# Moving matmul operands to other places in SBUF, counted in 64-byte units modulo four, in a one-core graph and attention layer

## The reference, cut to what matters

```
xn  = layernorm(x)
gnn = gather over dst of (xn @ weight), weighted by a softmax of attention sums over src and dst
Q, K, v = elu(xn@Wq)+1, elu(xn@Wk)+1, (xn@Wv)/L          # 8 heads of 32
msg = (Q @ (K^T v)) / (Q . sum K) * L @ Wm ; msg = layernorm(msg)*g1+b1
h   = relu(concat[xn, msg] @ W1) @ W2      # 512 -> 512 -> 256
x   = x + gnn + xn + layernorm(h)*g2+b2
z   = layernorm(x)
out = x + mlp(z; sW1, sW2, sW3) + top-2 of 4 experts(z; eW1, eW2, eW3), gated by softmax(z @ gW)
```

## The kernel before, in words

| tensors | used as | unit before | unit after |
|---|---|---|---|
| `w_hi`, `w_lo` | held under 512 columns, moving with 256 | 2 | 2 |
| `xT0` | moving, 512 | 0 | 2 |
| `xT1` | moving, 512 | 2 | 2 |
| `mT`, `s1` | moving, 512 | 3 | 2 |
| `z` | moving, 512; held under `g` | 3 | 2 |
| `rdenT` over `den_sel` | moving, 512, over held | 1 over 1 | 2 over 2 |
| `scaleT` over `gate_sel` | moving, 512, over held | 3 over 2 | 3 over 3 |
| `g` | moving, 256 | 2 | 1 |
| `h`, `s2_lo` | held under `w`, 256 | 3 | 3 |
| `s2_hi` | held under `w`, 256 | 1 | 3 |
| `wk` over `x1T` | moving, 256, over held | 2 over 3 | 2 over 3 |
| `wx` over `x1T` | moving, 264, over held | 2 and 0 over 3 | 2 over 3 |
| `xr` over `k` | moving, 258, over held | 0 and 2 over 1 | 2 over 3 |

## Time and profile before

### The profile page before, as it was taken

The page is one execution under the profiler, slowest core; times in us unless marked ns, Lnnn a source line. Parts: engine busy times, 40 slices in busy tenths (PEclk is TensorE's granted clock), DMA queues, the critical chain, the costliest instruction groups (busy, mean ns, idle before and its releaser), DMA issues.

```text
span 1326.4 us, 26270 instructions
## 1 busy us (share of the span) xinstructions
PE 1294.6 (98%) x8812; PEld 1121.4 (85%) x8812; DVE 1077.4 (81%) x2641; ACT 731.6 (55%) x1332; POOL 666.7 (50%) x771
## 2 busy tenths in 40 slices
PE   6999999898999999999999999999999999999998
PEld 6999999776888888888888888888888888888886
DVE  6888777978888888888888888888878888888875
ACT  4555555334645655555645655555645655555654
POOL 5777777746444453444444453444544453444421
PEclk9999999999999999999999999999999999999999
DMA  6787767522122221222121220222121220212000
GB/s 208 241 287 246 254 222 235 153 60 74 40 66 57 80 77 27 72 64 80 39 64 56 80 80 24 74 62 80 41 63 56 80 80 24 76 60 71 25 17 24
DMA packets 65460, 123.24 MB, mean 93 GB/s; under 512 B 31725, under 2 KB 36176, under 8 KB 65422
## 3 DMA queue, kind: packets, MB, share of 16 engines
q1 hardware_dynamic: 57422, 109.25, 25.5%
q0 software_dynamic: 8000, 13.53, 4.6%
HBM read 70.41 MB, written 52.32 MB: 93 GB/s over the span
## 4 chain that ended last, share of the span: by engine, by line
PE 88%; DVE 4%; issue 3%; ACT 2%; POOL 1%; POOLq 1%; DVEq 1%; ACTq 0%
PE psum L272 26%; PE psum L273 25%; PE psum L274 25%; PE psum L484 5%; PE psum L676 3%; PE psum L729 1%; PE psum L667 1%; PE psum L566 1%; PE psum L739 1%; PE psum L559 1%; POOLq L1780 1%; DVE s_lo L1516 0%; POOL ag L1842 0%; POOL xg L1840 0%; POOLq L1836 0%
## 5 line engine op out<-in xcount | busy, mean ns | idle before, releaser
L1846 POOL TENSOR_TENSOR h_lo<-relu,h_hi 128x1024 fp32r<-128x1024 f32 (+1 forms) x50 | 118.4, 2369 | 142.1 <-ACT h_hi L998 142.1
L272 PE MATMUL psum<-w_hi,h_hi 128*128 128x256 f32 x588 | 165.7, 282 | 4.9 <-ACT e L1009 3.1
L273 PE MATMUL psum<-w_lo,h_hi 128*128 128x256 f32 x588 | 165.0, 281 | 0.0
L274 PE MATMUL psum<-w_hi,h_lo 128*128 128x256 f32 x588 | 164.9, 281 | 0.0
L1846 POOL TENSOR_TENSOR s_lo<-relu,s_hi 128x512 fp32r<-128x512 f32 x23 | 29.6, 1289 | 206.0 <-ACT s_hi L1099 206.0
L272 PE MATMUL psum<-z_hi,w_hi 128*128 128x512 f32 (+1 forms) x300 | 121.6, 405 | 2.0 <-DVE z_lo L1616 1.1
L272 PE MATMUL psum<-xT_hi,w_hi 128*128 128x512 f32 (+1 forms) x300 | 118.9, 396 | 0.2 <-DVE relu L1556 0.2
L1840 POOL DMA_INDIRECT xg<-table_xt,idx x100 | 100.5, 1005 | 34.9 <-issue 33.2
L272 PEld LDWEIGHTS psum<-w_hi,h_hi 128*128 128x128 f32 x588 | 111.5, 190 | 7.1 <-ACT e L1009 3.3
L997 ACT ACTIVATE relu<-psum,h_bias 128x512 f32<-128x512 f32 (+1 forms) x100 | 67.8, 678 | 88.9 <-PE psum L274 88.8
L273 PE MATMUL psum<-z_lo,w_hi 128*128 128x512 f32 (+1 forms) x300 | 116.6, 389 | 0.0
(11 more groups left out here) (275 smaller groups left out, 4255.9 us busy)
## 6 DMA issues: line engine op xcount, KB each, us to landing
xb<-in_x SPq DMA_DIRECT2D x47, 448.0 KB, 3.9
xT_hi_table<-x1T_hi SPq DMA_DIRECT2D x25, 512.0 KB, 2.8
xT_lo_table<-x1T_lo SPq DMA_DIRECT2D x25, 512.0 KB, 3.6
xT_hi<-xT_hi_table SPq DMA_DIRECT2D x25, 512.0 KB, 3.8
xT_lo<-xT_lo_table SPq DMA_DIRECT2D x25, 512.0 KB, 4.8
table_xt<-xts SPq DMA_DIRECT2D x24, 455.0 KB, 3.0
out<-xmid SPq DMA_DIRECT2D x24, 448.0 KB, 2.9
xb<-in_x SPq DMA_DIRECT2D x47, 64.0 KB, 4.1
```

What stands on the lines that cost most here:

```text
L272: pe.matmul(out, wh, xh, start=first, stop=False)
L273: pe.matmul(out, wh, xl, start=False, stop=False)
L274: return pe.matmul(out, wl, xh, start=False, stop=last)
L1846: ptt(out, src, hi, ALU.subtract).then_inc(S[done], 1)
```

## The change

`side` now takes a unit modulo 4 instead of a parity, with up to three filler lines, and the count starts at 2, so that it is the unit of the address. Four names take the place of MOVING and HELD: WIDE = 2 (tensors that move with 512 columns, and the weights), HELD = 3 (held under 256 columns), KEYS = 1 and KEYS_HELD = 2 (`g`, and `z` which is held under it). Some tensors get a side that had none. The pitch of `wx` and `xr` grows from 288 to 320 floats, so that each of their parts starts at the same unit. No instruction is added, removed or moved to another place in an engine's order.

```diff
-MOVING, HELD = 0, 1
+FIRST = 2
+WIDE, HELD, KEYS, KEYS_HELD = 2, 3, 1, 2
-XA_PITCH = KX_PITCH = 288
+XA_PITCH = KX_PITCH = 320
-        used = [0]
+        used = [FIRST]
             lines = -(-4 * math.prod(shape[1:]) // LINE)
-            if side is not None and used[0] % 2 != side:
-                stack.enter_context(nc.sbuf_tensor(name + "_side", [P, LINE // 4], F32))
-                used[0] += 1
+            off = 0 if side is None else (side - used[0]) % 4
+            if off:
+                stack.enter_context(nc.sbuf_tensor(name + "_side", [P, off * LINE // 4], F32))
+                used[0] += off
...
-        w_hi = sb("w_hi", [P, W_TOTAL], F32R, side=MOVING)
-        w_lo = sb("w_lo", [P, W_TOTAL], F32R, side=MOVING)
-        out_bias = sb("out_bias", [P, C], F32R, side=MOVING)
-        gate_sel = sb("gate_sel", [P, 2, P], F32R)
+        w_hi = sb("w_hi", [P, W_TOTAL], F32R, side=WIDE)
+        w_lo = sb("w_lo", [P, W_TOTAL], F32R, side=WIDE)
+        out_bias = sb("out_bias", [P, C], F32R, side=WIDE)
+        gate_sel = sb("gate_sel", [P, 2, P], F32R, side=HELD)
...
-        g_hi = sb("g_hi", [P, CK, C], F32R, side=MOVING)
+        g_hi = sb("g_hi", [P, CK, C], F32R, side=KEYS)
...
-        xT_hi0 = sb("xT_hi0", [P, CK, GR], F32R)
+        xT_hi0 = sb("xT_hi0", [P, CK, GR], F32R, side=WIDE)
...
-        den_sel = sb("den_sel", [P, CK, P], F32R)
+        den_sel = sb("den_sel", [P, CK, P], F32R, side=WIDE)
...
-        rdenT = sb("rdenT", [P, GR], F32R)
+        rdenT = sb("rdenT", [P, GR], F32R, side=WIDE)
...
-        z_hi = sb("z_hi", [P, CK, GR], F32R, side=HELD)
+        z_hi = sb("z_hi", [P, CK, GR], F32R, side=KEYS_HELD)
...
-        s1_hi = sb("s1_hi", [P, 2, GR], F32R)
+        s1_hi = sb("s1_hi", [P, 2, GR], F32R, side=WIDE)
...
-        mT_hi = sb("mT_hi", [P, CK, GR], F32R)
+        mT_hi = sb("mT_hi", [P, CK, GR], F32R, side=WIDE)
...
```

More of the change, by code:

```diff
@@ L126, in gps_layer @@
         ident = sb("ident", [P, P])
-        w_hi = sb("w_hi", [P, W_TOTAL], F32R, side=MOVING)
-        w_lo = sb("w_lo", [P, W_TOTAL], F32R, side=MOVING)
-        out_bias = sb("out_bias", [P, C], F32R, side=MOVING)
-        gate_sel = sb("gate_sel", [P, 2, P], F32R)
+        w_hi = sb("w_hi", [P, W_TOTAL], F32R, side=WIDE)
+        w_lo = sb("w_lo", [P, W_TOTAL], F32R, side=WIDE)
+        out_bias = sb("out_bias", [P, C], F32R, side=WIDE)
+        gate_sel = sb("gate_sel", [P, 2, P], F32R, side=HELD)
         gate_w = sb("gate_w", [P, CK, QUAD])
         second_w = sb("second_w", [P, EXPERTS, HEAD_CH])
-        g_hi = sb("g_hi", [P, CK, C], F32R, side=MOVING)
-        g_lo = sb("g_lo", [P, CK, C], F32R, side=MOVING)
+        g_hi = sb("g_hi", [P, CK, C], F32R, side=KEYS)
+        g_lo = sb("g_lo", [P, CK, C], F32R, side=KEYS)
         g2_bc = sb("g2_bc", [R, C])
@@ L169, in gps_layer @@
         row_n = sb("row_n", [R, T, C])
-        xT_hi0 = sb("xT_hi0", [P, CK, GR], F32R)
-        xT_lo0 = sb("xT_lo0", [P, CK, GR], F32R)
+        xT_hi0 = sb("xT_hi0", [P, CK, GR], F32R, side=WIDE)
+        xT_lo0 = sb("xT_lo0", [P, CK, GR], F32R, side=WIDE)
         qf = sb("qf", [P, CK, GR])
@@ L174, in gps_layer @@
         low_rows = sb("low_rows", [P, QUAD + 1])
-        den_sel = sb("den_sel", [P, CK, P], F32R)
+        den_sel = sb("den_sel", [P, CK, P], F32R, side=WIDE)
         ctx1, before_ctx1 = ExitStack(), used[0]
         w_raw = sb("w_raw", [P, W_TOTAL], stack=ctx1)
[L180 to L183, removed]
+        wk_hi = sb("wk_hi", [P, CK, C], F32R, stack=ctx1, side=WIDE)
+        wk_lo = sb("wk_lo", [P, CK, C], F32R, stack=ctx1, side=WIDE)
+        wx_hi = sb("wx_hi", [P, CK, XA_PITCH], F32R, stack=ctx1, side=WIDE)
+        wx_lo = sb("wx_lo", [P, CK, XA_PITCH], F32R, stack=ctx1, side=WIDE)
         x1T_hi = [sb(f"x1T_hi{n}", [P, CK, GR], F32R, stack=ctx1, side=HELD) for n in range(2)]
@@ L196, in gps_layer @@
         xn1 = [sb(f"xn1_{n}", [R, T, C], stack=ctx1) for n in range(2)]
-        xr_hi = [sb(f"xr_hi{n}", [R, T, KX_PITCH], F32R, stack=ctx1, side=MOVING) for n in range(2)]
-        xr_lo = [sb(f"xr_lo{n}", [R, T, KX_PITCH], F32R, stack=ctx1, side=MOVING) for n in range(2)]
+        xr_hi = [sb(f"xr_hi{n}", [R, T, KX_PITCH], F32R, stack=ctx1, side=WIDE) for n in range(2)]
+        xr_lo = [sb(f"xr_lo{n}", [R, T, KX_PITCH], F32R, stack=ctx1, side=WIDE) for n in range(2)]
         kf = [sb(f"kf{n}", [R, T, C], stack=ctx1) for n in range(2)]
@@ L221, in gps_layer @@
         ag = [sb(f"ag{n}", [R, T, HEADS]) for n in range(2)]
-        xT_hi = [xT_hi0, sb("xT_hi1", [P, CK, GR], F32R)]
-        xT_lo = [xT_lo0, sb("xT_lo1", [P, CK, GR], F32R)]
+        xT_hi = [xT_hi0, sb("xT_hi1", [P, CK, GR], F32R, side=WIDE)]
+        xT_lo = [xT_lo0, sb("xT_lo1", [P, CK, GR], F32R, side=WIDE)]
         h_hi = sb("h_hi", [P, 4, GR], F32R, side=HELD)
         h_lo = sb("h_lo", [P, 4, GR], F32R, side=HELD)
-        z_hi = sb("z_hi", [P, CK, GR], F32R, side=HELD)
-        z_lo = sb("z_lo", [P, CK, GR], F32R, side=HELD)
-        s1_hi = sb("s1_hi", [P, 2, GR], F32R)
-        s1_lo = sb("s1_lo", [P, 2, GR], F32R)
+        z_hi = sb("z_hi", [P, CK, GR], F32R, side=KEYS_HELD)
+        z_lo = sb("z_lo", [P, CK, GR], F32R, side=KEYS_HELD)
+        s1_hi = sb("s1_hi", [P, 2, GR], F32R, side=WIDE)
+        s1_lo = sb("s1_lo", [P, 2, GR], F32R, side=WIDE)
         scaleT = sb("scaleT", [P, GR], F32R, side=HELD)
-        mT_hi = sb("mT_hi", [P, CK, GR], F32R)
-        mT_lo = sb("mT_lo", [P, CK, GR], F32R)
+        mT_hi = sb("mT_hi", [P, CK, GR], F32R, side=WIDE)
+        mT_lo = sb("mT_lo", [P, CK, GR], F32R, side=WIDE)
         s2_lo = sb("s2_lo", [P, GR], F32R, side=HELD)
```

## The result

The changed kernel took 1331.8 us in the median of 15 runs (1325.7 to 1333.6), the kernel before, in 15 runs beside it, 1325.9 (1320.9 to 1327.0). The ratio is 1.0039, with a 95% interval of 1.0025 to 1.0053: slower by about 5 us, where 8.4 us less was forecast (1315, in a range of 1308 to 1320). The profiled execution took 1332.01 us with a span of 1330.3, against 1328.16 and 1326.4 before.

The account below looks back on a forecast made before the run. The prediction took the spacing of PE's matmuls as the bound. Gains of 4.0 (512 columns), 3.2 (W2) and 1.2 us (phase 1), 8.4 in all, took the median from 1323.7 to a predicted 1315 us, range 1308 to 1320.

Parts of the forecast that it names:

- What bounds the kernel: Phase 2: PE never waits in turns 3 to 23, so only the spacing of matmuls sets the span.
- The 512-column term: Phase 2 matmuls on `xT0`, `mT`, `z`, `s1` become equal pairs, 2 over 2; 4.0 us gained.
- The mark of 42.25 us a turn: Turn length in phase 2 that the profile after would show if the forecast was right.
- The W2 term: W2 in phase 2 falls into the fast spacing behind eW1 on `z`, now an equal pair; 3.2 us gained.
- The other 256-column sections add nothing to this: Phase 2's 256-column sections besides W2 were priced at nothing, since turns differ by 0.165 us in all.
- Phase 1: `wx` and `xr` at new units gain a quarter of at most 4.7 us: 1.2 us, lower bound nothing.
- A: Rival for all matmuls: placement does not matter, time stays at 1323.7 us; chance 0.09.
- the rule quoted beside it: TensorE has two independent read ports, so loading next weights takes no bandwidth from the running matmul; the change does nothing.
- C: Rival: W2 stays as it is, or `z` is no equal pair because the period exceeds four units; 1318.5 us, chance 0.17.
- D: Rival: phase 1 wins all of its 4.7 us, giving 1311.8 us; chance 0.12.
- B: Rival: phase 2's 256-column sections and `wk` tip into the slow spacing; 4.6 us slower, 1328 us; chance 0.07.
- the two reads collide: In PE, reads of moving and next stationary operand collide at some offsets, about 4 ns in each matmul.

Follow-up runs that it names:

- b_xm: Kernel before with only `xT0` and `mT` moved to unit 2; 1322.3 us in rounds, ratio 0.9952.
- b_z: Kernel before with only `z` moved to unit 2 and `g` to 1; 1325.56 us once, beside 1323.3.
- a_s2: Changed kernel with `s2_hi` back at unit 1; 1333.3 us once, beside 1326.55 of the kernel before.
- b_s2: Kernel before with only `s2_hi` moved, from unit 1 to 3; 1335.1 us once.
- b_x: Kernel before with `xT0`, `mT`, `s1`, `rdenT`, `den_sel` at unit 2; 1324.41 us once; timed in rounds as b_x_timed, 1324.1 us, ratio 0.9971.
- u0_pairs: Layer left out: only matmul triples on zeros, moving unit 2 or 1 over held units 0 to 7; spacings measured, 113.3 to 120.0 ns at 256 columns.
- before_again: Kernel before, unchanged, profiled a second time; its 21 turns took 892.20 us.
- a_mix: Changed kernel with `s2_hi` and `h_lo` at unit 1 and `g_lo` at 3; 1323.7 us in rounds, ratio 0.9969.
- a_gate: Changed kernel with `gate_sel` back at unit 2; 1337.87 us once.
- after_again: Changed kernel, unchanged, run again; 1332.4 us in rounds against the kernel before, ratio 1.0030.

## Why the prediction was wrong

*What bounds the kernel*: right. The whole of the difference in the turns is in the spacing of PE's matmuls, and VectorE's time, 739.83 for 739.60 us, hardly changed. What failed are two terms of the sum: W2, entered with the wrong sign, and the other 256-column sections, entered at nothing.

*The 512-column term*, 4.0 us: right, a little large. 0.141 us a turn are 3.4 us over 24, and the parts are `xT` 1.1 (priced 1.8), `mT` 0.7 (1.0), `z` 1.2 (1.0) and the rest 0.4. The marks came out: 2.72 us for 12 on Wq in even and odd turns. Wq alone gives 1.1 us, nearly all of `xT`. What is missing against the price is not the pairs' own: in b_xm, where `xT0` and `mT` alone move, they gain 1.9 and 1.3 us. In the changed kernel it is missing where sections start afresh. The 12 matmuls on `mT` behind the transposes take 2.850 us (before 2.846, b_xm 2.821), W1 parts 0 and 1 behind the slow `g` 2.764 (before 2.761, b_xm 2.746). In turn 11 the 11 matmuls from 689.87 to 692.40 take 230.0 ns each, and the 12 behind them 226.7. eW1's last 17 take 3.90 us as before, not 3.88. (The mark of 42.25 us a turn was a slip besides: 42.585 less 7.2 / 24 is 42.285.)

*The W2 term*, 3.2 us gained: wrong, and in its sign. "If the entry decides, W2 falls into the fast spacing behind it" was half right. The entry decides, as b_z shows with W2's own operands in place; but the equal pair in front leads into the slow spacing. The step took "fast in front" for "fast behind" on no row at all. W2 in turn 11 before stood behind the same 3 over 2 as in turn 14, so no row told which entry leads where. It measured 0.059 us a turn lost, 1.4 us over 24, close to the bound that the text named (1.6 us), which had as much right to be the value as the gain had.

*"The other 256-column sections add nothing to this"*: the costliest error. It was read from the turns of before, where these sections differ little from turn to turn. That says that they had one spacing there, not that they would keep it. They were all fast, and their being fast hung on things that the change took away. For the output product that is shown in both directions by a_s2 and b_s2: 0.15 us a turn, from one held tensor that 8 of the 40 matmuls read. `g` tips when `z` and `g` alone move (b_z), and also when neither of its operands moves (b_x, b_xm), 0.09 us a turn each time. Together 0.237 us a turn, 5.7 us in the span, entered at nothing.

*Phase 1*, 1.2 us gained: wrong by 1.5 us. `wx` and `xr` over their new pairs have the spacing of before, and the turn is 0.014 us longer. The step scaled 2 over 3 at 256 columns to 258 and 264; no row supported the scaling, and the fact that the step itself named, that half of `wx` stood at 2 over 3 already "and the section is none the faster", spoke against it. The lower bound of nothing was the value to take.

*The rivals.* A falls: the pairs differ by up to 7.5 ns with nothing else changed. And it is the pair that counts: held unit 0 is among the slowest under moving unit 2 (120.0 ns) and among the fastest under moving unit 1 (113.3). So the rule quoted beside it, the Trainium skill, "TensorE: Matmul & The Clock Gate", section "Step-by-step: what each phase is for", does not describe these matmuls: with separate ports that took nothing from each other, u0_pairs would show one spacing for each width. C falls: u0_pairs speaks against its period of eight, `z` at its new place gained 1.2 us, and W2 did not stay as it was; D falls with phase 1. B, at a chance of 0.07, is what happened. It priced 1920 tipped matmuls at 7.9 us against a gain of 4.0, and nearly all of them tipped: 0.296 us a turn, 7.1 us over 24, against 3.4. Only its further 1.9 us for `wk` did not come. It gave 4.6 us and the trace shows 3.9 in the span.

The rounds show some 5.2 us (1325.9 x 0.0039), more than these 3.9. An estimate of the rest: against before_again, where W2 is mostly fast, the difference of the turns would be 897.40 - 892.20 = 5.2 us. If most executions of the kernel before are nearer to that one than to the profiled one, nothing more has to be explained; but only two of them were seen in a trace, so this is not shown.

So what is shown is this. In this kernel a 256-column section of these triples has two spacings, 113.3 to 114 and 117.5 to 118 ns, at the same addresses, and mostly holds the one it is in. Which it gets depends on what ran in front of it, and a held tensor at another unit inside it can throw it into the fast one. Before, `s2_hi` at unit 1 was such a break, among `scaleT`, `s2_lo` and `h` at 3. The change made all held tensors of the output product equal, and it led into W2 and `g` by other entries.

What stays open: why `g` isn't freed by its break in a_mix (only `g_lo` was shifted, a moving tensor, where the breaks that worked were held ones; a held one, `z_lo`, wasn't tried); which of `s1`, `rdenT` and `den_sel` tips `g`; why u0_pairs, on zeros, has 2 over 3 in the slow spacing behind either entry; what makes W2 choose in the kernel before; and what the passage's 107.6 to 120.0 us hang on. In a_s2, a_gate and b_s2 ScalarE waited 12.0 us there before the copy into `g_hi`, elsewhere 6.0 to 7.5, with no cause found; these three were taken side by side on one chip, and the kernel before took 1326.55 us there, without a profile. No run tested what the two reads do inside the engine, so "the two reads collide" remains a picture.

## What to carry to other kernels

A spacing read from a trace belongs to a section with its neighbours, not to its pair of addresses. Where one placement shows two spacings, price every section of that kind at both of them, those whose operands don't move too. Move the tensors of one product at a time and read the spacing of all the others after each step; here the part with the clean rows, two tensors, measured 0.5% faster, and the full scheme cost 0.4%. And take the mark from a stretch in which the bounding engine never waits: 21 such turns of the changed kernel repeated to 0.2 us, where single times of the same kernel lay 8 us apart.

## What was not expected of the hardware

- The effect of the held operand's place repeats after four units of 64 bytes, and the pair that is best at one width is worst at another: 2 over 2 has 226.7 ns at 512 columns, the lowest of the four, and 120.0 at 256, as high as any. 1 over 2, at 256, has 113.3 alone and 117.5 in the changed kernel.
- An equal pair at 512 columns reaches its spacing only after a run-in behind transposes: after the first matmul, seven more at 230.0 ns in u0_pairs and eleven in turn 11 of the changed kernel, then 226.7.
- Two 256-column sections with several others between them can flip together: in b_x_timed, turn 23, the spacings of W2 and of `g` are both the opposite of what they are in the 20 other turns.
- In the passage between the phases, where PE has waits, the granted clock fell from 2.4 to 1.2 GHz, the lower of its two levels, for 3.4 to 17.1 us in all, and in after_again not at all. In the window from 254 to 335 us the profile of the changed kernel shows a mean clock of 0.94 and 424 matmuls, after_again, the same kernel, 1.00 and 462.
